# Issuing the write of A's diagonal blocks from ScalarE's DMA queue instead of SyncE's

## The reference

```python
q = silu(dw_causal_conv(h @ Wq, conv_q_w))      # h: layer-normed x; the same for k and v
delta_out, _ = delta_rule_chunkwise(q4, k4, v4, sigmoid(h @ Wb))
local_out = dw_causal_conv(v, local_w)           # 7 taps
mid_out = dw_causal_conv(v, mid_w)               # 25 taps

# in delta_rule_chunkwise: 4 heads, chunks of 32 tokens
T = -einsum('bhnid,bhnjd->bhnij', kb * 1, k)     # kb = beta * k, k of unit length
T = where(tri_strict, T, 0.0)
for i in range(1, c):                            # forward substitution: the inverse of a unit triangle
    T = T.at[..., i, :i].add(einsum('bhnj,bhnji->bhni', T[..., i, :], T[..., :, :i]))
```

## Time and profile before

| | us |
|---|---|
| median of 3 runs | 8387.36 |
| lowest, highest | 8381.74, 8402.19 |
| the profiled execution | 8374.86 |
| its span, first to last instruction | 8373.1 |
| busy: TensorE, VectorE, ScalarE, GpSimd | 7421.8, 4866.4, 3367.4, 1783.2 |

### The profile page before, as it was taken

How to read it: one execution, slowest core, us unless ns; L and a number is a source line. 1 busy time by engine, 2 the same in 40 slices (tenths; PEclk the granted TensorE clock), 3 DMA queues, 4 the chain that set the end, 5 groups by cost and what they waited for, 6 DMA issues and landing times. The chain is left out here.

```text
span 8373.1 us, 122632 instructions
## 1 busy us (share of the span) xinstructions
PE 7421.8 (89%) x47710; PEld 4285.2 (51%) x47710; DVE 4866.4 (58%) x9426; ACT 3367.4 (40%) x6875; POOL 1783.2 (21%) x2689
## 2 busy tenths in 40 slices
PE   6899988989888998888988899888888888998898
PEld 4546455464554645546455464554645546455464
DVE  5465664656646566564665656656466564665646
ACT  2252533525335253352533525335253352534425
POOL 2112121121211222112121122211222112221221
PEclk9999999999999999998999999999999999999999
DMA  2021111101112011120111202111021110211102
GB/s 72 16 38 24 32 46 23 42 13 32 46 24 44 10 32 46 24 44 10 32 46 24 44 10 37 41 29 42 8 37 41 32 46 1 37 41 31 46 2 41
DMA packets 337786, 268.71 MB, mean 32 GB/s; under 512 B 213521, under 2 KB 276369, under 8 KB 337097
## 3 DMA queue, kind: packets, MB, share of 16 engines
q1 hardware_dynamic: 337148, 260.09, 15.3%
HBM read 48.71 MB, written 42.02 MB: 11 GB/s over the span
## 5 line engine op out<-in xcount | busy, mean ns | idle before, releaser
L1791 ACT ACTIVATE sa_pt<-ps 128x512 f32<-128x512 f32 (+3 forms) x3072 | 1271.9, 492 | 728.8 <-PE ps L1779 723.3
L1716 DVE TENSOR_REDUCE sa_nm<-ps 128x2 f32<-128x1024 f32 (+4 forms) x1280 | 1389.1, 1114 | 281.5 <-PE ps L1697 138.1
L1779 PE MATMUL ps<-sa_qs,sa_ks 99*128 99x512 bf16 (+3 forms) x3072 | 795.8, 333 | 76.3 <-ACT sa_pt L1791 58.3
L1798 POOL TENSOR_SCALAR_AFFINE_SELECT sa_pt<-sa_pt 128x512 f32<-128x512 f32 x512 | 325.2, 635 | 1703.1 <-ACT sa_pt L1791 1700.6
L1697 PE MATMUL ps<-sa_ks,sa_qs 96*128 96x512 bf16 (+3 forms) x2560 | 631.0, 321 | 57.5 <-DVE sa_nm L1716 36.9
L1811 PE MATMUL ps<-sa_pt,sa_va 128*17 128x512 f32 (+3 forms) x6144 | 644.9, 492 | 8.2 <-POOL sa_pt L1798 8.2
L312 PE MATMUL ps<-identb 128*128 128x512 bf16 x2608 | 626.9, 388 | 10.4 <-ACT dr_z L1061 10.4
L1779 PEld LDWEIGHTS ps<-sa_qs,sa_ks 99*128 99x128 bf16 x3072 | 257.8, 97 | 651.9 <-ACT sa_pt L1791 473.6
L609 PE MATMUL ps<-rep,stack 128*32 128x512 f32 x4608 | 529.2, 611 | 41.9 <-DMA rep<-paths 41.9
L280 POOL TENSOR_TENSOR rstd<-vare,mhalf 128x2 f32<-128x2 f32 x260 | 181.0, 696 | 1248.5 <-DVE vare L272 1248.5
L857 POOL TENSOR_TENSOR A<-paths 128x256 f32<-128x256 f32 x384 | 271.9, 740 | 799.7 <-DVE paths L1027 799.7
(11 more groups left out here) (353 smaller groups left out, 14070.1 us busy)
## 6 DMA issues: line engine op xcount, KB each, us to landing
sa_qs<-sa_parts SPq DMA_DIRECT2D x288, 128.0 KB, 5.0
sa_ks<-sa_parts SPq DMA_DIRECT2D x288, 128.0 KB, 5.8
x<-in_x SPq DMA_DIRECT2D x17, 1024.0 KB, 5.6
rep<-paths SPq DMA_DIRECT2D x128, 128.0 KB, 2.4
bounce<-paths SPq DMA_DIRECT2D x32, 512.0 KB, 2.8
out_y<-x SPq DMA_DIRECT2D x32, 512.0 KB, 3.0
rep<-paths SPq DMA_DIRECT2D x128, 127.9 KB, 2.4
rep<-paths SPq DMA_DIRECT2D x128, 127.8 KB, 3.2
```

What stands on the lines that cost most here:

```text
L1716: nc.vector.tensor_reduce(nm[:, g % 2, op.c, op.t, op.j:op.j + op.heads], cols, AX.X, ALU.max, negate=True).then_inc(s.slot_free, 1)
L1779: last = nc.tensor.matmul(bank[:, off:], ks[0:QROWS, g % NBUF, j, kt * P:(kt + 1) * P], qs[0:QROWS, g % NBUF, j, n * BANK + off:(n + 1) * ...
L1791: nc.scalar.activation(pt[:, gs % 2, j, off:BANK], ring_bank(ring_use(gs, j))[:, off:], ACT.Exp, scale=RATIO).then_inc(s.ring_out, 1)
L1798: nc.gpsimd.affine_select(block, block, [[0, GH], [1, P]], ALU.is_ge, 0.0, base=0, channel_multiplier=-1).then_inc(s.masked, 1)
```

## The change

The 4 transfers of A's blocks leave SyncE's list and go into ScalarE's, between `first_tap(2, 1)` and `to_token_major(0)`, with the wait for A in front. SyncE goes from `copies(0)` straight on to the first half of `copies(1)`; its wait for `s.blocks_out` stays.

```diff
             copies(0, range(SHIFTS))
-            sp.wait_ge(s.a, T)
-            for b in range(BLOCKS):
-                part = slice(CHUNK * b, CHUNK * (b + 1))
-                sp.dma_start(bounce[0, b].rearrange("g r c -> r g c"),
-                             by_blocks(A, P)[part, :, part]).then_inc(s.blocks_out, 16)
             copies(1, range(SHIFTS // 2))
             sp.wait_ge(s.blocks_out, 16 * BLOCKS)
...
             evacuate(2, 1)
             first_tap(2, 1)
+            act.wait_ge(s.a, T)
+            for b in range(BLOCKS):
+                nc.scalar.dma_start(bounce[0, b].rearrange("g r c -> r g c"),
+                                    by_blocks(A, P)[rows(b), :, rows(b)]).then_inc(s.blocks_out, 16)
             to_token_major(0, m.k_tm[:])
             to_token_major(1, m.v_tm)
             silu(2, 0)
```

## The result

| | before | after |
|---|---|---|
| median of 12 runs (lowest to highest) | 8398.60 us (8377.81 to 8418.18) | 8434.26 us (8405.95 to 8459.30) |
| ratio, 95% interval | | 1.0043 (1.0026 to 1.0060) |
| profiled execution, its span | 8374.86, 8373.1 us | 8405.95, 8404.2 us |
| TensorE busy, share | 7421.8, 89% | 7452.2, 89% |

The change makes the kernel slower by 0.43%, some 36 us; the two profiled spans stand 31.1 us apart. The forecast was 8392 us with a range to 8425 and "no difference" as the likeliest case. The time lies outside that range, on the side that had a chance of 0.23.

A forecast was written before the change was run, and what follows sets the result against it. The prediction took the forward substitution's inverse as the bound, with TensorE's late small product deciding in 11 of 16 sequences. Terms of -13 and +18 us gave +5: 8380 us profiled, 8392 against the median, range 8360 to 8425.

The forecast's parts named there:

- no difference: Whole kernel: time stays within 0.3%, 25 us, of before; chance 0.64.
- the side that had a chance of 0.23: Whole kernel: slower than before by more than 0.3%, 25 us.
- SyncE's gain: SyncE's copies run on without a gap; `block_a` is issued 0.9 us sooner and the copies are complete at 2718.1.
- ScalarE's issues: Four issues of A's blocks on ScalarE take 2.6 us, so the copies of turned tiles begin 3.4 us later.
- the rival: ScalarE's issues each wait behind one of SyncE's copies: 4.5 us, +2.7 us a sequence, 8431 us; chance 0.20.
- My own bound from above: Upper limit for ScalarE's four issues of A's blocks together: 4.5 us.
- TensorE's gap: Ahead of turning v, TensorE idles 2.7 us where it had no gap, with a clock fall in 11 of 16.
- the term of +18 us: Ahead of turning v: clock falls in 11 of 16 sequences at 1.6 us each, +18 us.
- VectorE's chain "does not move": VectorE's substitution starts at 2714.45 against 2714.40 before; the sums' later start eats the wait for `block_a`.
- Unit 2: Convolutions on TensorE: copies of v hidden, idle time of 2.5 us and clock fall gone; takes 6.2 us at full clock.
- The end of the stage: Behind the inverse: the loads follow it step by step, so the shift is carried on as it is.
- -13: At the pick, small product 1.2 us sooner in 11 sequences and 0.1 later in 5: -13 us.

The follow-up runs named there:

- Two other kernels: Kernel before plus 10 warming matmuls ahead of unit 2: 8358.45 us, 1.0003; kernel before with SyncE issuing copies(1) transfers as 4, 6 and 6: 8351.85 us, 0.9992.

## Why the prediction was wrong

**SyncE's gain: right.** Copies without a gap, `block_a` issued 0.9 us sooner on average (22.14 to 21.23 us after the first copy), its wait covered. The two copies issued beside ScalarE's issues took 1.5 us longer together, which I had not reckoned with and which cost nothing.

**ScalarE's issues: the step that failed.** "The nearest rows are SyncE's own issues of the same four transfers ... I take 2.6." Those rows were taken with nothing in flight: SyncE had waited 2.88 us, and its copies were through. Stretches of TensorE's engine windows (columns as above), before, just ahead of the issues at 2700.36:

```profile
2698.50:2699.50 1.00, 1.00 (x15) 1.00 0.15 37
2699.50:2700.40 0.90, 0.90 (x11) 1.00 0.00 0
```

After, while ScalarE issues:

```profile
2710.50:2711.50 1.00, 0.00 (x0) 1.00 0.73 169
2711.50:2712.50 1.00, 0.00 (x0) 1.00 0.96 158
```

The DMA engines stood at 0 GB/s then and move 158 to 169 now. I had even written that copies were still to be moved at 2700.4 in the changed kernel, and priced the issues by rows without them. The row that warned stood in the trace: the copy issued behind A's blocks, 1.76 us. I gave it to the rival and priced the forecast by the others. Sixteen copies at 0.63 us a piece beside moving copies, which I set against it, proved no guard: they were issued with nothing of A's under way. Beside or behind A's issues a copy is held up as well, 1.32 and 1.42 us in the changed kernel and 1.6 to 2.2 before. Why a copy is not held up by other copies was not tried. My own bound from above, 4.5 us, held, as did the points that I had given: the lead is lost at 3.5 us, 0.3% is passed at about 3.8.

**TensorE's gap: right place, too small.** 2.7 us forecast, 4.2 measured, 1.4 of the difference from the issues. A share of falls was a fair forecast for such a gap, but 11 of 16 was a guess that happened to lie between what gaps of 2.85 and 2.97 us showed, 7 and 15. At 4.2 it fell in 16. The price of a fall, 1.6 us, measured 1.7 in turning v of the sequence shown (3.61 less 1.91) and 1.8 on average at the inverse (53.91 less 52.09). With 16 falls instead of 11 the term of +18 us becomes 16 x 1.8 = 29.

**VectorE's chain "does not move": wrong.** Its sums start 4.2 us later in the sequence shown (24.80 against 20.59 after the first copy) where I had 2.0: 1.4 from the issues, and 0.9 because ScalarE's copies of turned v wait for a TensorE at half clock (4.88 us for the eight copies, 4.0 forecast). The wait for `block_a` covers 2 us of it and no more, so the substitution starts at 29.09 instead of 27.08. I had not thought that a fall of TensorE's clock would come back to VectorE through ScalarE; with the clock kept full there, the substitution starts 0.9 us sooner (28.22). Yet it is TensorE's chain that sets the time. In all 16 sequences VectorE waits for the small product, 21.3 us in all, where it waited in 11 before, 16.8 us:

```profile
  PE ps L533: 21.3, 16
```

**Unit 2: right.** No wait, no fall, 6.19 us.

**The end of the stage: wrong.** "I carry the shift on as it is." Falls there went from 7 to 11 of 16, and taking them away gives back 0.8 us a sequence. Two other kernels show it more clearly: a gain of 1.0 and 2.1 us at the inverse came out as 0.3 and 0.8 at the next stage.

**The sum as measured.** Of the 40 us by which the stretch is longer, 29 are the falls ahead of turning v and 13 those at the end of the stage; the rest of the change is -2 (62.93 less 63.04, times 16): the gain on SyncE's side and the falls that are gone, 11 ahead of unit 2 and 6 at the end, just pay for the late copies. I had -13 and +18.

**The rival.** Its size was right, 8431 against 8434.26, and its price of the issues too, 4.5 against 3.97. Its mechanism was not: six issues of SyncE's beside ScalarE's left them at 2.71 us, and behind SyncE's last copy they were lengthened all the same (3.2 to 4.1). What it had right is that the two queues hold each other up. The Trainium skill ("Perfetto Trace Analysis", DMA Instruction — HWDGE) describes a generator of descriptors shared by two sequencers and locked for an issue. Beside small issues no run here shows such a lock between SyncE and ScalarE (2.71 us against 2.59); whether it has a part in what large transfers do, no run tells. The Trainium skill's other rule ("DMA: Bandwidth & Descriptors", Issuing engines are not separate DMA queues), that several issuing engines save the time of the issue only, agrees with `block_a` here, which came 0.9 us sooner where SyncE was spared 2.6 us of issue; what decided here was what the issues cost the engine that took them over, 3.97 us.

## What to carry to other kernels

Price a DMA issue by a row in which as much is in flight as will be after the change, and ask what stands behind it on the engine that takes it: ahead of copies that TensorE waits for it is paid twice, once as a wait and once by TensorE's clock. A queue's wait is better filled with that queue's own next transfers than by giving work to another engine: that gave 0.5% here where the change lost 0.4%. And when idle time of TensorE is moved or taken away, count the falls of the clock at every later wait too, since one that is gone may come back further on.

## What the runs showed of the hardware

- The time of an issue depends on what is under way. A's four transfers of 128 KB each took 2.59 us to issue with nothing beside them on either queue, 2.71 beside six tiny issues of the other queue, 3.97 beside copies that SyncE went on issuing, 3.2 to 4.1 behind the last of these, and 4.16 beside one transfer of 512 KB. On SyncE's own queue, right behind its own copies, they took 2.62 to 2.67 in 13 of 16 sequences and up to 4.20 in the others.
- The hold-up also meets the issues of the other queue and those that follow: a copy takes 0.59 us to issue beside other copies, 1.32 and 1.42 beside ScalarE's issues of A's blocks, and 1.6 to 2.2 behind them on one queue.
- TensorE's granted clock fell from 1.00 to 0.50 behind gaps of 4.2 us in 16 of 16 sequences, behind gaps of 2.85 us in 7 and of 2.97 us in 15 of 16, and behind gaps of 0.9 to 1.7 us, ahead of unit 2 in the kernel in which SyncE fills its wait, in none. The length alone does not decide: ahead of unit 2 in the kernel before it fell behind gaps of 2.4 to 3.0 us in 11 sequences and stayed full behind gaps of 2.1 to 2.9 us in 5.
- At the end of the stage it fell in 1 to 16 of 16 sequences in kernels that differ there in nothing. With the earlier falls gone it was 16 of 16 in two kernels, and 1 and 4 in two others. What decides there stays open.
